# Three steps of VectorE's order and GpSimd's bias moved in a fused attention and Hadamard-MLP kernel

## What is computed

```python
x = L0_attn_x                                   # 8 sequences of 1024 tokens, 512 wide, float32
x = x + attn(layernorm(x))
x = x + ffn(layernorm(x))

def attn(x):
    c  = (x @ W_to_kv.T) @ W_compress.T          # 64 wide
    ch = layernorm(c) * ln_gamma + ln_beta
    q, k, v = ch @ W_q_comp.T, *split(ch @ W_kv_comp.T)
    q, k = rope(q), rope(k)
    o = softmax(causal(q @ k.T / 8)) @ v
    z = o @ W_comp2lat.T
    return z @ W_to_kv + z @ W_out_res.T + b_out_res

def ffn(x):                                     # W1, W3: 2048 x 512, W2: 512 x 2048
    hidden = silu(x @ W1.T) * (x @ W3.T)
    return fwht(hidden) @ W2.T                  # Walsh-Hadamard transform over 2048
```

## Time and profile before

| | |
|---|---|
| median of 3 runs (lowest to highest) | 2167.86 us (2167.37 to 2168.67) |
| the profiled execution: its time, its span | 2166.91 us, 2165.1 us |
| granted clock of PE over the span, as a share | 0.986 |
| PE matmuls busy | 2078.7 us, 96% of the span |
| DVE busy | 1443.1 us, 67% |
| ACT busy | 951.1 us, 44% |
| POOL busy | 196.6 us, 9% |

### The profile page before, as it was taken

The page is one execution under the profiler, slowest core; times in us unless marked ns, Lnnn a source line. Parts: engine busy times, 40 slices in busy tenths (PEclk is TensorE's granted clock), DMA queues, the critical chain, the costliest instruction groups (busy, mean ns, idle before and its releaser), DMA issues. The chain is left out here.

```text
span 2165.1 us, 27021 instructions
## 1 busy us (share of the span) xinstructions
PE 2078.7 (96%) x9884; PEld 985.4 (46%) x9884; DVE 1443.1 (67%) x2774; ACT 951.1 (44%) x1453; POOL 196.6 (9%) x196
## 2 busy tenths in 40 slices
PE   6678989999999999999999999999999999999999
PEld 3434444444444444444444444444444444444444
DVE  7887787766667576765767666775767667653343
ACT  6846545343543534444443435434343444432221
POOL 2233443000000000000000000000000000000000
PEclk8889999999999999999999999999999999999999
DMA  8435324633346324633246333454236333363112
GB/s 324 159 117 201 128 83 149 175 121 118 108 126 169 123 78 118 168 129 125 72 138 168 108 114 120 127 159 136 75 116 166 119 121 101 90 167 116 69 71 76
DMA packets 231141, 278.65 MB, mean 129 GB/s; under 512 B 178016, under 2 KB 178144, under 8 KB 225632
## 3 DMA queue, kind: packets, MB, share of 16 engines
q1 hardware_dynamic: 231008, 276.91, 41.2%
HBM read 194.81 MB, written 39.85 MB: 108 GB/s over the span
## 5 line engine op out<-in xcount | busy, mean ns | idle before, releaser
L842 PE MATMUL PF<-XF,WS 128*128 128x512 f16 x1792 | 684.5, 382 | 16.5 <-DVE PF L1812 9.4
L843 PE MATMUL PF<-XF,WS 128*128 128x512 f16 x1792 | 682.3, 381 | 0.0
L844 PE MATMUL PF<-XF,WS 128*128 128x512 f16 x1792 | 681.8, 380 | 0.0
L866 PE MATMUL PD<-W2S,H 128*128 128x512 f16 x1024 | 388.1, 379 | 0.0
L867 PE MATMUL PD<-W2S,H 128*128 128x512 f16 x1024 | 388.1, 379 | 0.0
L868 PE MATMUL PD<-W2S,H 128*128 128x512 f16 x1024 | 388.1, 379 | 0.0
L1217 ACT ACTIVATE SH<-PF,afs 128x512 f32<-128x512 f32 x256 | 175.9, 687 | 382.5 <-PE PF L844 378.1
L842 PEld LDWEIGHTS PF<-XF,WS 128*128 128x128 f16 x1792 | 175.6, 98 | 254.4 <-issue 37.1
L1834 DVE TENSOR_TENSOR H<-SH,H 128x1024 f16<-128x1024 f32 x128 | 156.7, 1224 | 178.9 <-ACT H L1228 178.9
L844 PEld LDWEIGHTS PF<-XF,WS 128*128 128x128 f16 x1792 | 176.1, 98 | 213.4 <-issue 3.6
L1826 DVE SCALAR_TENSOR_TENSOR SH<-PF,afs,SH 128x512 f32<-128x512 f32 x256 | 191.5, 748 | 114.5 <-ACT SH L1217 100.6
(11 more groups left out here) (317 smaller groups left out, 2060.9 us busy)
## 6 DMA issues: line engine op xcount, KB each, us to landing
WS<-wscr SPq DMA_DIRECT2D x112, 896.0 KB, 4.9
W2S<-w2scr SPq DMA_DIRECT2D x30, 1024.0 KB, 6.5
ring<-x SPq DMA_DIRECT2D x56, 256.0 KB, 7.0
wscr<-WS SPq DMA_DIRECT2D x16, 896.0 KB, 3.7
out<-ring SPq DMA_DIRECT2D x56, 256.0 KB, 2.4
XF<-w SPq DMA_DIRECT2D x16, 512.0 KB, 7.4
RAW<-w13t SPq DMA_DIRECT2D x16, 512.0 KB, 3.9
xraw<-xT SPq DMA_DIRECT2D x28, 256.0 KB, 5.6
```

The source lines that it names most:

```text
L842: pe.matmul(bank, wh, th, start=i < 2 and j == 0, stop=False, skip_group_check=True)
L843: pe.matmul(bank, wh, tl, start=False, stop=False, skip_group_check=True)
L844: m = pe.matmul(bank, wl, th, start=False, stop=j == 1, skip_group_check=True)
L866: pe.matmul(PD[:, t % 2, :], th, wh, start=j == 0, stop=False)
```

## The change

In VectorE's loop, `sum_c(k)` goes in front of `low_part(k - 1)` and of the odd tile's `out_rows`, and `fill(k, 1)` goes in front of all three. In GpSimd's program the four bias additions of a half go from slots 8 and 9 to slots 12 and 13.

```diff
                 fill(k, 0)
+                fill(k, 1)
+                sum_c(k)
                 if k:
                     low_part(k - 1)
-                fill(k, 1)
-                if k:
                     out_rows((k - 1) // 4 - 1, 2 * ((k - 1) % 4) + 1)
-                sum_c(k)
                 if k == 0:
                     tokens_sum(0, 6)
                 fill(k, 2)
...
             def attention(a, slot):
-                if slot in (8, 9):
-                    bias(a, (2 * slot - 16, 2 * slot - 15))
+                if slot in (12, 13):
+                    bias(a, (2 * slot - 24, 2 * slot - 23))
```

## The result

The changed kernel takes 2176.57 us (median of 6 runs, 2173.49 to 2178.61) against 2167.88 for the kernel before (median of 6, 2167.32 to 2168.67): 8.7 us more, a ratio of 1.0040 with a 95% interval of 1.0029 to 1.0050. The forecast was 2164.4 with a range up to 2169.3, so the change went the other way. The profiled execution of the changed kernel is the slowest of its six, 2178.61 us, 11.7 over the one profiled before.

What follows compares the result with a forecast made beforehand. PE is busy end to end, so its waits bound the kernel, the largest for `sum_c` (9.4 us). Gains of 0.8 (stages 1 to 6) and 3.7 (stage 0) less 1.0 (stage 7) give 2167.86 - 3.5 = 2164.4 us, range 2158.5 to 2169.3.

Steps and rivals of the forecast that it cites:

- blocks 3, 9, 15: the late sums: Stages 1 to 6: the earlier sum ends PE's waits at product 4, 1.48 us a stage, 8.9 us gained.
- block 0: L609: Stages 1 to 6: seventh form and conv come later on VectorE, PE's projection waits 0.79 us, 4.7 us lost in six.
- block 6: L609: Stages 1 to 6: ScalarE's silu waits for the later low part, conv and projection shift 0.57 us, 3.4 us in six.
- stage 7: The seventh form comes 1.80 us later, block 1's weights behind it in SPq have 0.79 us of room; 1.0 us lost.
- stage 0, block 8 to the end of 9: Second half's first norm: GpSimd's later bias ends the collision and V comes earlier; 4.9 us gained, bounds 0 and 5.9.
- Most blocks have this room: Stages 1 to 6: 1.80 us of low part and output rows fit behind the sum, except in blocks 0 and 6.
- In stages 1 to 6 attention matmuls stretch the block and leave room.: Block 1's weights behind the later seventh form in SPq's program cost only in stage 7, 1.0 us; nothing in stages 1 to 6.
- Stage 0 together: 4.9 - 0.5 + 0.7 - 1.4 = 3.7 us gained.: Second half's norm gains 4.9, first half's loses 0.5, block 15's late sum gains 0.7, block 9 loses 1.4 us.
- The prediction's other figure, 3.6: Stage 0's second-half norm gain if block 7's low part waits up to 1.3 us more beside a bias addition.
- The slower rival: Block 2, stages 1 to 6: product 2 waits for the late hidden half, 5.4 us lost, 2169.8 us; chance 0.1.
- The covers: Rival: ScalarE and VectorE absorb the later low part in blocks 0 and 6, saving half or more of 8.1 us; chance 0.25.
- The collisions in stage 0: Rival: bias additions still meet the norm's root, the 4.9 us gain is 0, 2169.3 or 2167 us; chance 0.2.

Runs made afterwards that it cites:

- e3: The changed kernel with VectorE's order of before in block 0 of every stage; 2169.11 us, ratio 1.0011.
- e4: The kernel before with VectorE's new order in blocks 3, 5, 9 and 15 of stages 1 to 7 alone; 2158.79 us, ratio 0.9958.
- e5: The kernel before with VectorE's new order in blocks 3, 5, 9, 15 of stages 1 to 7 and GpSimd's bias in slots 12 and 13; 2154.49 us.
- e7: The changed kernel with VectorE's order of before in stage 0 and in blocks 0, 1, 6 and 11 of the other stages; 2153.62 us.
- e8: The changed kernel with the seventh form's low half between sum and low part in block 0 of stages 1 to 7; 2176.86 us.
- e10: The changed kernel, new order only in blocks 3, 9, 15 (stage 0: 15), stage 1's attention input loads issued before the seventh form's transposition; 2150.78 us.
- e2: The kernel before with GpSimd's part of the change alone, bias additions in slots 12 and 13; 2162.68 us, ratio 0.9979.
- e6: The changed kernel with VectorE's order of before in all of stage 0; 2169.07 us.
- e11: The changed kernel, new order only in blocks 3, 9, 15 (stage 0: 15), bias of stage 0's first half back in slots 8 and 9; 2152.05 us.
- e12: The changed kernel with the low part back in front in all blocks, fill 1 and sum before the odd tile's output rows alone; 2154.26 us, ratio 0.9940.
- e1: The changed kernel with GpSimd's bias back in slots 8 and 9, so VectorE's part alone; 2177.31 us, ratio 1.0045.

## Why the prediction was wrong

Point by point, the forecast's terms and what the two traces show (stages 1 to 6 summed; the rows of stage 0 from product to product, "end of 9" being the start of block 9's last product):

| term | forecast, us | measured, us |
|---|---|---|
| blocks 3, 9, 15: the late sums | -8.9 | -9.2 |
| block 5 | 0 | 0 |
| block 0: L609 | +4.7 | +4.2 |
| block 6: L609 | +3.4 | +2.9 |
| block 11: L663 | none | +3.5 |
| block 2: product 2; block 12 | none | +1.5; +0.8 |
| stage 1: SyncE's loads, and the half clock | none | +1.2, and +1.4 |
| stage 5: half clock, this execution | none | +1.7 |
| stage 7 | +1.0 | +1.0 |
| stage 0, block 8 to the end of 9 | -4.9 | -3.9 |
| stage 0, blocks 4 to 7 | none | +1.6 |
| stage 0, rest of 9 to 12 | +1.4 | +2.3 |
| stage 0, first four blocks | +0.5 | +3.9 |
| stage 0, behind it | -0.7 | -0.5 |

The measured terms come to 12.4 us, the stages' differences to 11.8; the rest is shifts of under 0.1 us each and block 5 of stage 5, which gave back less. Against the forecast's -3.5 they are 15.9 us too many: 7.1 in stage 0, 5.8 in blocks 2, 11 and 12, 2.6 in stage 1, 1.7 by stage 5's clock, less 1.3 by which the late sums and L609's two terms came out better. Between the medians the error is 12.2 us.

The terms of stages 1 to 7 that were worked out from rows came within 0.5 us each, also in the runs that took them one by one (e3, e4, e5). (Block 6's walk gives 0.53 us a stage by its own figures, the sum has 0.57, the trace 0.43.) The bias in stages 1 to 6 does nothing, as said. The mechanism was right where it was applied; the sum was wrong because it was not complete. Three steps failed, each a term put at nothing or nearly so.

**"Most blocks have this room: `sum_e` is needed only four steps later. Two have not."** The step looked at PE's next product and at the conv. It didn't go through every instruction that stands behind the sum on VectorE, and every one behind `silu` on ScalarE, with the one that waits for it. L1591 in block 11 is such a one: it frees a PSUM buffer. Block 1 passes its delay on to block 2's product 2, where the rival had 0.85 us of delay for 0.9 of room; in stage 3 the copy L1206 came 1.17 us later in the block, and product 2 lost 0.25. The prediction named a wait of that product for L1206 as a sign of being wrong, and it came, small as it is. With block 12 these are 5.8 us, over a third of the error by the trace. e7 shows that these blocks, with 0 and 6, are all that cost in stages 1 to 6.

**"In stages 1 to 6 attention matmuls stretch the block and leave room."** That holds for the weights of block 1, and not of what else stands behind the seventh form in SyncE's queue. In stage 1 that is the load of the attention's inputs, which PE already waited for: the kernel before has the wait (the longest of L609's, 2.2 us, is in stage 0; the one in stage 1 is 1.26), so it had no room at all. A later transposition could only add to it. 1.2 us, or 2.6 with the clock; e3 and e8 bring it back, and e10 takes away even the part that was there before.

**"Stage 0 together: 4.9 - 0.5 + 0.7 - 1.4 = 3.7 us gained."** It lost 3.4. GpSimd's part fell short by 1 us. Without ScalarE's copy of V the walk had 5.9 us (4.1, 0.8 and 1.0), and e2, which has the order of before, shows 5.0, because block 9's product 2 now waits for L1206. The copy of V was booked at 1.0, and between e2 and the changed kernel the same stretch is 1.1 us longer, with L644's wait of 1.42. So 3.9 us were gained there instead of 4.9. The prediction's other figure, 3.6, had the low part up to 1.3 us later beside a bias addition. It met one that was near its end and took 0.46 us longer, and these 0.46 lie in ScalarE's path to L644.

The larger failure is that the other blocks of stage 0 were dismissed with one term for block 9. e6 shows that VectorE's order costs 7.5 us in stage 0 by the medians and 6.65 by the trace, where the terms had 1.7 (1.0 for the copy of V, 1.4 for block 9, less 0.7). L609, L622 and `pv` each wait some 0.6 us more in blocks 6 and 7, the same kinds of wait as in later stages, and L622 in block 1 waits 1.8 us more: there the whole delay of the low part reaches PE through ScalarE's queue. Of the first four blocks as a whole: with the order and bias of before they took 84.3 and 83.1 us in two profiles, and 84.5 in e11, whose bias there is the one before; with the new bias alone 83.3 to 86.2 in six, with VectorE's new order 85.8 to 88.3 in four. The bias' share, some 1 us, isn't told apart from the scatter.

That is also why the two parts don't add when both are whole: GpSimd's move wins 4.7 us by itself and only 0.7 on top of VectorE's new order (2177.31 to 2176.57). Some 3.4 of these missing 4 us are in blocks 8 and 9: the new order alone brings their 36.6 us down to 34.3, with V waited for 2.72 us instead of 3.92, so that GpSimd's move finds 1.5 us left to win instead of 5.0. The rest is open.

The slower rival was given 0.1, at 2169.8, with one mechanism of 0.9 us in block 2. It was the right side for too narrow a reason: its own mechanism gave 1.5 us, and others of the same kind outweighed it. The covers did not hold. The collisions in stage 0 moved in small part only, to V's last operations and the low part.

## What to carry to other kernels

When a piece of work moves back in an in-order queue, list everything between its old place and the next idle time of that engine, with each one's consumer and its room, and do the same for the engine that waits for the moved piece and for the DMA queue behind what is delayed; the piece that another engine waits for (here the low part) is seldom the one to move. Moving only what few wait for (the output rows, e12) gave the same gain with nearly none of the cost, and changing the order only in the three blocks that had a late sum did as well. A load that PE already waits for has no room: in stage 1 whatever delayed its issue was paid, in e12 too.

## What was not expected of the hardware

The same wait is followed by the lower clock in one kernel and not in the next. PE's L609 in stage 1 waited 2.24 us in the changed kernel, with a granted clock of 0.66 over the 5 us behind it, and 2.40 us in e1, with 1.00. `pv` in stage 5 waited 2.06 us and was followed by 0.57 over 4 us, in e1 2.23 us with 1.00. Here are the two windows of the changed kernel's and of e1's stage 5, in that order:

```profile
1506.00:1510.00 4.00, 4.00 (x13) 1.84 (x11) 1.11 (x3) 2.02 (x3) 0.00 (x0) 0.57 0.43 151
```

```profile
1503.00:1507.00 4.00, 3.88 (x23) 2.21 (x24) 1.89 (x4) 2.28 (x3) 0.00 (x0) 1.00 0.63 200
```

The fourteen profiles have fifteen waits of 2.0 us or more at these two places. Behind six of them (2.05, 2.06, 2.06, 2.24, 2.51 and 2.60 us: two in the changed kernel, one each in e4, e5, e6 and e8) the clock fell to 1.2 GHz, behind the other nine (2.01 to 2.49) it did not, nor behind any shorter one there (1.25 to 1.97). Each such stretch cost 1.4 to 1.7 us, so a wait that a change lengthens by 0.2 us can cost that much more. This may be one reason why the changed kernel scatters over 5.1 us in six runs where the one before scattered over 1.4 beside it; it isn't shown, and beside the experiments the kernel before, with more runs, spread from 2163.4 to 2170.5.

VectorE's operations on SBUF beside GpSimd's additions behaved alike in four kernels: L1435 on 128x4 takes 0.16 us alone and 1.20 behind the start of a bias addition (before, e1), L1513 on 128x256 0.42 in e2 and 1.37 in the changed kernel beside the row of four. The Trainium skill, SBUF — State Buffer, section Who interferes with whom, has such a pair exclude each other for an instruction's length; these rows agree with it.
